# Moving the second layer's keys from the opening of a two-layer attention and mixture-of-experts kernel into its router and expert stages

## The reference, cut to what matters

```python
# x: [2, 512, 256]   ctx: [2, 1024, 256]   16 heads of 16
x = x + attention0(layernorm(x), ctx, mask)          # Wq0, Wk0, Wv0, Wo0 and biases
x = x + moe_capacity(layernorm(x))                   # router, top 2 of 8 experts, capacity 32 a group
x = x + attention1(layernorm(x), ctx, pad, attn_mask) # Wq1, Wk1, Wv1, Wo1 and biases
x = x + moe_top2(layernorm(x))                       # 8 experts, top 2
# in both attentions
q = y @ Wq.T + bq;  k = ctx @ Wk.T + bk;  v = ctx @ Wv.T + bv
out = softmax(mask(q k^T / 4)) v @ Wo.T + bo
```

## Time and profile before

| | |
|---|---|
| runs (3) | 1237.43, 1238.1 (median), 1240.68 us |
| the profiled execution | 1238.72 us, span 1237.0 us |
| busy | PE 1145.1, PEld 732.2, DVE 544.9, ACT 450.2, POOL 244.2 us |
| opening | 0 to 87 us |
| attention 0 with its projection | 88 to 340 us |
| router stage, expert stage | 341 to 380 us, 380 to 627 us |
| attention 1 with its projection, top-2 mixture | 628 to 941 us, 942 to 1237 us |

### The profile page before, as it was taken

One profiled execution on the slowest core, in us unless ns is written; L12 is line 12 of the kernel. 1 busy time (PEld: TensorE's weight loads), 2 busy tenths in 40 slices (PEclk: granted clock), 3 DMA queues, 4 the chain that ended last, 5 costly groups with the idle time before them and its releaser, 6 DMA issues. The chain is left out here.

```text
span 1237.0 us, 19157 instructions
## 1 busy us (share of the span) xinstructions
PE 1145.1 (93%) x7215; PEld 732.2 (59%) x7239; DVE 544.9 (44%) x1553; ACT 450.2 (36%) x591; POOL 244.2 (20%) x366
## 2 busy tenths in 40 slices
PE   6989999999859999999779999999987699999996
PEld 4443333333447888888656333333326699999995
DVE  4657777773362111121157776666406322212111
ACT  4556666666422111111143455555652101110110
POOL 4652222225000000000004000000200233333331
PEclk9999999999959999999989999999998799999998
DMA  8646222001172333345349221120004599999971
GB/s 224 166 150 159 42 40 43 3 1 50 53 273 51 136 136 136 136 147 195 65 180 210 38 39 39 40 40 1 1 1 160 202 372 377 314 321 310 318 231 47
DMA packets 87926, 168.53 MB, mean 136 GB/s; under 512 B 9474, under 2 KB 61396, under 8 KB 85252
## 3 DMA queue, kind: packets, MB, share of 16 engines
q1 hardware_dynamic: 80132, 157.99, 40.5%
q0 software_dynamic: 5152, 6.05, 2.5%
q10 hardware_dynamic: 2560, 3.41, 1.0%
HBM read 147.30 MB, written 20.98 MB: 136 GB/s over the span
## 5 line engine op out<-in xcount | busy, mean ns | idle before, releaser
L1213 ACT ACTIVATE prob<-st_ps 128x1024 f32<-128x1024 f32 x256 | 253.8, 1022 | 186.9 <-PE st_ps L1095 105.0
L219 DVE CUSTOM_DVE_ANT_0 junk<-s_ps,bias_rows,mx 128x512 f32<-128x512 f32 x236 | 167.8, 748 | 64.0 <-PE s_ps L204 63.3
L1087 PE MATMUL st_ps<-q_stack,k_stack 100*128 100x512 bf16 x512 | 183.7, 382 | 7.6 <-ACTq L1188 3.5
L219 DVE CUSTOM_DVE_ANT_0 junk<-s_ps,bias_rows 128x512 f32<-128x512 f32 x232 | 153.3, 689 | 66.0 <-PE s_ps L204 65.5
L204 PE MATMUL s_ps<-k_stack,q_stack 97*128 97x512 bf16 x468 | 174.9, 383 | 7.3 <-ACT q_stack L248 5.4
L1600 PE MATMUL h_ps<-expert_in,w 128*128 (+1 forms) x704 | 155.0, 382 | 2.2 <-PEq L66 2.2
L1600 PEld LDWEIGHTS h_ps<-expert_in,w 128*128 128x128 f32 (+1 forms) x704 | 132.7, 189 | 23.0 <-issue 2.4
L1107 PE MATMUL o_ps<-prob,v_unit 128*32 128x512 f32 x1024 | 139.7, 599 | 1.0 <-ACT prob L1213 1.0
L204 PEld LDWEIGHTS s_ps<-k_stack,q_stack 97*128 97x128 bf16 x468 | 44.8, 98 | 140.2 <-DVE mx L219 83.8
L1946 ACT ACTIVATE silu<-gu_ps 128x512 f32<-128x512 f32 x46 | 27.5, 597 | 227.1 <-PE gu_ps L1887 227.1
L1630 ACT ACTIVATE gelu_out<-h_ps 128x256 f32<-128x256 f32 (+1 forms) x88 | 33.7, 383 | 182.2 <-PE h_ps L1600 182.2
(11 more groups left out here) (283 smaller groups left out, 1185.3 us busy)
## 6 DMA issues: line engine op xcount, KB each, us to landing
wg<-in_gateT SPq DMA_DIRECT2D x23, 1024.0 KB
wu<-in_upT SPq DMA_DIRECT2D x23, 1024.0 KB
wd<-in_downT SPq DMA_DIRECT2D x23, 1024.0 KB
w<-in_w SPq DMA_DIRECT2D x16, 1368.0 KB
w<-in_w SPq DMA_DIRECT2D x8, 1280.0 KB
k_scr<-k_parts SPq DMA_DIRECT2D x48, 128.0 KB, 2.3
k_stack<-k_scr SPq DMA_DIRECT2D x16, 384.0 KB, 4.9
k_stack<-k_scr SPq DMA_DIRECT2D x16, 256.0 KB, 5.6
```

The costliest lines, as they stand in the source:

```text
L219: self.pr.nc.vector.tensor_tensor_reduce(out=self.junk[:, self.bank("job", u, j)], in0=self.ps[:, self.bank("job", u, j)], in1=self.m.bias ...
L1087: pe.matmul(st_ps[:, h], stack(K[b], ROWS, i % 2, h, slice(kt * P, (kt + 1) * P)), stack(Q[b], ROWS, i % 2, h, slice(0, SQ)), start=True, ...
L1213: nc.scalar.activation(prob[:, kt % 2, 2 * hp:2 * hp + 2], st_ps[:, 2 * hp:2 * hp + 2], ACT.Exp).then_inc(exp_done, 1)
```

## The change

The opening has 12 cells, with the second half of the queries as cells 6 and 7 and `NA = 8`; the first layer's last four key cells come in four rounds of five row jobs, one cell and one value tile, and four rounds of three jobs and two value tiles follow. Only 4 value tiles stand ahead of the loop (`OWN`), 12 are copied by ACT without bias, and POOL adds it later. Four row jobs of unit 1 (`EARLY`) are done ahead instead of 12. The second layer's key weights and `ctxT` are loaded in the last unit of attention 0 into buffers that are free by then (`K[0]`, `V[0]`), its 8 key cells are multiplied in the router stage between PE's other work, and POOL splits them in the expert stage, where SP sends them out and reads two stacks back before it loads the third expert's weights.

```diff
@@ opening, order of the cells
-        cells = [("k", 0, 0, 0), ("k", 0, 0, 1), ("q", 0, 0, 0), ("k", 0, 0, 2), ("k", 0, 0, 3), ("q", 0, 0, 1)]
-        cells += [("k", 0, 1, ch) for ch in range(4)] + [("q", 0, 1, 0), ("q", 0, 1, 1)]
-        cells += [("k", 1, dt, ch) for dt in range(DT) for ch in range(4)]
+        cells = [("k", 0, 0), ("k", 0, 1), ("q", 0, 0), ("k", 0, 2), ("k", 0, 3), ("q", 0, 1)]
+        cells += [("q", 1, 0), ("q", 1, 1)] + [("k", 1, ch) for ch in range(4)]
-        NA = 6
+        NA = 8
+        OWN = 4
-            return JOBS[PER * r:PER * (r + 1)] if r < NC - NA - 1 else JOBS[PER * r:]
+            return JOBS[5 * r:5 * r + 5] if r < 4 else JOBS[20 + 3 * (r - 4):23 + 3 * (r - 4)]
@@ opening, SP
-                sp.dma_start(wk_raw[1], t["wkT1"].rearrange("(t p) n -> p t n", p=P)).then_inc(wk_in[1], 16)
-                bias_in(sp, bk[:, 1], t["bk1"], wk_in[1])
...
-                for dt in range(DT):
-                    for b in range(B):
-                        for i in (2 * dt, 2 * dt + 1):
-                            k_out_of(1, i, b, 12 + 4 * dt + 2 * b + 1)
@@ opening, POOL, behind the last split
+                pool.wait_ge(v_kept, NV // 2 - OWN)
+                g.tensor_tensor(m.vals[:, OWN:NV // 2], m.vals[:, OWN:NV // 2],
+                                m.bv[:].unsqueeze(1).broadcast_to([P, NV // 2 - OWN, D]), ALU.add).then_inc(v_sum, 1)
+                top.cut(pool, row, 1)
@@ opening, PE
                 cell(5)
+                cell(6)
+                cell(7)
                 pe.wait_ge(wv_in, 32)
-                for n in range(NV // 2):
+                for n in range(OWN):
                     value(n)
...
-                    row.scores(pe, jobs[:1])
-                    cell(NA + r, (1,))
-                    row.scores(pe, jobs[1:])
+                    row.scores(pe, jobs[:2])
+                    cell(NA + r, (0,))
+                    row.scores(pe, jobs[2:4])
+                    cell(NA + r, (1,))
+                    row.scores(pe, jobs[4:])
+                    value(OWN + r)
+                for r in range(4):
+                    jobs = jobs_of(4 + r)
+                    row.scores(pe, jobs[:1])
+                    value(2 * OWN + 2 * r)
+                    row.scores(pe, jobs[1:])
+                    value(2 * OWN + 2 * r + 1)
+                    if r == 1:
+                        top.turn(pe, 0)
+                pe.wait_ge(pr.load[0][1], 16 * N_DMA)
+                row.scores(pe, NEXT[:3])
+                top.turn(pe, 1)
+                row.scores(pe, NEXT[3:])
+                pe.wait_ge(hi_done, NA + 2)
+                pe.wait_ge(full_done, 2)
+                for n in range(4):
+                    pe.matmul(kq_ps[:, 0, 0:D], pr.ident[:], ctxT[:, 0, 0:D], start=True, stop=True)
@@ attend, layer 0
-        plan = row_plan(AHEAD if l == 0 else 0)
+        plan = row_plan(EARLY if l == 0 else 0)
@@ attend, SP, layer 0
+                    sp.wait_ge(st_ready, (NU - 1) * 16)
+                    sp.dma_start(pr.late_ctx(), t["ctxT"].rearrange("(t p) n -> p t n", p=P)).then_inc(pr.late_in, 16)
+                    sp.wait_ge(pv_done, 2 + (NU - 1) * KT)
+                    sp.dma_start(pr.late_wk()[0], t["wkT1"].rearrange("(t p) n -> p t n", p=P)).then_inc(pr.late_in, 16)
+                    bias_in(sp, pr.late_bk, t["bk1"], pr.late_in)
                     sp.wait_ge(cut_done, KT)
@@ moe_capacity, router stage, PE
+                    key_cell(0)
+                    key_cell(1)
                     norm.tensor(pe, tps, logits)
+                    key_cell(2)
+                    key_cell(3)
                     pe.wait_ge(m1_done, 1)
@@ moe_capacity, router stage, ACT
+                    def key_out(n):
+                        act.wait_ge(k_ready, n + 1)
+                        bias = pr.late_bk[:, n // 4:n // 4 + 1]
+                        nc.scalar.activation(pr.late_part(n, 0), kps[:, n % 3], ACT.Identity, bias=bias)
+                        nc.scalar.activation(pr.late_full(n), kps[:, n % 3], ACT.Identity, bias=bias).then_inc(full_done, 1)
-                    norm.scalar(act, tps)
+                    norm.scalar(act, tps, first_keys)
                     act.wait_ge(x_sub, 1)
                     nc.scalar.activation(raw[:], raw[:], ACT.Exp).then_inc(x_exp, 1)
+                    for n in range(2, NK):
+                        key_out(n)
@@ moe_capacity, expert stage, SP
+                for dt in range(DT):
+                    for b in range(B):
+                        sp.wait_ge(late_low, 4 * dt + 2 * b + 2)
+                        for i in (2 * dt, 2 * dt + 1):
+                            keys_out(pr, sp, 1, pr.late_parts(), pr.late_out, i, b)
+                sp.wait_ge(pr.late_out, 16 * 3 * NG * B)
                 for b in range(B):
                     k_stack(pr, sp, 1, 0, b)
@@ moe_capacity, expert stage, POOL (new)
+                def split(n):
+                    rest = pr.late_full(n)
+                    g.tensor_tensor(rest, rest, pr.late_part(n, 0), ALU.subtract).then_inc(late_step, 1)
+                    pool.wait_ge(late_step, 2 * n + 1)
+                    g.tensor_copy(pr.late_part(n, 1), rest).then_inc(late_step, 1)
+                    pool.wait_ge(late_step, 2 * n + 2)
+                    g.tensor_tensor(pr.late_part(n, 2), rest, pr.late_part(n, 1), ALU.subtract).then_inc(late_low, 1)
```

More of the change, by code:

```diff
@@ L399, in split_done, with k_out_of @@
                     sp.wait_ge(lo_done, n + 1)
-                def k_out_of(l, i, b, last):
+                def k_out_of(i, b, last):
                     split_done(last)
-                    keys_out(pr, sp, l, k_parts, k_out[l], i, b)
+                    keys_out(pr, sp, 0, [k_parts[:, p] for p in range(3)], k_out[i][b], i, b)
                 def q_out_of(i, b, last):
@@ L481, in cell @@
                 def cell(n, ks=range(DT)):
-                    kind, l, dt, ch = cells[n]
-                    w, src = (wk[:, l], ctxT) if kind == "k" else (wq, pr.yT)
+                    kind, dt, ch = cells[n]
+                    w, src = (wk, ctxT) if kind == "k" else (wq, pr.yT)
                     for k in ks:
@@ L626, in _ @@
                         middle(n - 1)
-                    if n - NA == 10:
+                    value_kept(OWN + n - NA)
+                middle(NC - 1)
+                for n in range(2 * OWN, NV):
+                    value_kept(n)
+                    if n == 2 * OWN + 4:
                         top.write(act, 0)
-                middle(NC - 1)
                 top.write(act, 1)
@@ L692, in _ @@
                 dve.wait_ge(wv_in, 32)
-                for n in range(NV // 2):
+                for n in range(OWN):
                     value_out(n)
-                for r in range(NC - NA):
+                for r in range(8):
                     row.maxima(dve, jobs_of(r))
-                for n in range(NV // 2, NV):
-                    value_out(n)
+                row.maxima(dve, NEXT)
 class NormSteps:
@@ L808, in q_stack, with keys_out @@
                      src[:, 0:n]).then_inc(pr.load[l][b], 16)
-def keys_out(pr, sp, l, parts, done, i, b):
+def keys_out(pr, eng, l, parts, done, i, b):
     dst = scratch(pr, "k_scr", l, i, b, SK)
@@ L815, in keys_out @@
     for p in range(3):
-        sp.dma_start(dst[:, p], parts[at:at + HG * DH, p, i // 2, b * SK:(b + 1) * SK]).then_inc(done[i][b], 16)
+        eng.dma_start(dst[:, p], parts[p][at:at + HG * DH, i // 2, b * SK:(b + 1) * SK]).then_inc(done, 16)
 def queries_out(pr, sp, l, m, i, b):
@@ L1431, in logits, with key_cell @@
                         mm.then_inc(l_ready, 1)
+                    def key_cell(n):
+                        dt, ch = divmod(n, 4)
+                        if n == 0:
+                            pe.wait_ge(pr.late_in, 64)
+                        if n >= 3:
+                            pe.wait_ge(full_done, n - 2)
+                        for k in range(DT):
+                            mm = pe.matmul(kps[:, n % 3], wk[:, k, dt * P:(dt + 1) * P],
+                                           ctx[:, k, ch * 512:(ch + 1) * 512], start=(k == 0), stop=(k == DT - 1))
+                        mm.then_inc(k_ready, 1)
+                    key_cell(0)
+                    key_cell(1)
                     norm.tensor(pe, tps, logits)
+                    key_cell(2)
+                    key_cell(3)
                     pe.wait_ge(m1_done, 1)
```

156 lines of the change are left out of this document (100 added, 56 removed).

## The result

The changed kernel took 1226.6 us (median of four runs, 1220.6 to 1228.1) against 1238.1 before: a ratio of 0.9883 with a 95% interval of 0.9862 to 0.9903. Two later series gave 0.9865 (0.9841 to 0.9890) and 0.9873 (0.9847 to 0.9898). Forecast were 1224 us, a range of 1217 to 1231, and a gain of over 0.3% with a chance of 93%. The profiled execution took 1228.0 us (span 1226.3, against 1237.0 of before).

The account below looks back on a forecast made before the run. PE, or chains through it, was taken to bound the opening and attention, while the router stage had room. Terms 0.7 - 15.4 + 1.75 - 0.9 + 0 - 0.5 + 0 = -14.3 us gave 1224 us, range 1217 to 1231.

Parts of the forecast that it names:

- Part 1: Opening ahead of the loop: two more query cells delay the third value tile; cost 0.7 us, between 0 and 2.
- Part 2: Opening's loop and tail: 33.3 us in place of 48.7, so -15.4 us, bounds -10 and -17.
- Part 3: Attention: eight more row jobs in unit 0 cost 1.75 us, less half clock at its start saves 0.9.
- Part 4: Attention's end: late loads on SP's queue, some 17 us, cost nothing; if late, up to 5 us.
- Part 5: Router stage: key cells between PE's other work, earlier logits, faster dispatch; sum -0.5 us.
- dispatch itself: Router stage: dispatch matmuls, 9.81 us before, are 6.9 at full clock, but DVE feeds them every 1.2 us: -1.9.
- The -4.6 of a full clock: Router stage: the gain in us if the clock stayed full throughout; as a rival, 17%, total 1220 us.
- rows 9: Profile rows of the second mixture's router stage: clock falls to 0.52 amid transposes and logits though PE counts as busy.
- Part 6: Expert stage: POOL's splits and SP's sends delay the third expert's weights, with 5 us of slack: cost nothing.
- The slower-side rival: Expert stage: POOL at half speed, splits take 51 us, third expert's weights late, PE waits 20 us: 1244 us; 4%.

Follow-up runs that it names:

- DVE's other order: Changed kernel with DVE's row bias behind the first two value outputs and ahead of the last two, not ahead of all four; 1225.1 us, ratio 0.9879.
- the thin cells: Kernel before the change, the second layer's eight key cells in the opening multiplying 8 columns instead of 512; 1240.0 us against 1242.4, ratio 0.9988.
- the 2, 2, 2, 2 order: The changed kernel's own placement of the router stage's eight key cells, two in each of four places, the first ahead of the transposes; 1226.6 us.
- the one profile with full clock throughout: Changed kernel with one key cell cut in halves inside the logits, then 1, 1, 2 cells and one inside dispatch; 1222.8 us.

## Why the prediction was right, point by point

The sum was -14.3 us, the profile has -10.7. The sign, the range and the mechanism of the large term held. The 3.6 us that are missing are 1.1 in part 1 (where the starts of the two profiles fell), 0.9 in part 2, 2.0 in part 5, and -0.1 and -0.2 in attention and behind the router stage.

- **Part 1, ahead of the loop (+0.7).** The third value tile waits for DVE by 3.60 us ("some 4"), and the two tiles behind it take 2.4 us and not 3.4. But the loop starts at 40.86, not 39.9, as the first value tile is at 32.95 and 30.7 was expected (27.25 of before and two cells). The mean of the first value tile's start is 31.6 us over the twelve profiles with the changed opening and 28.2 over the two of before's (27.25 and 29.19): 3.4 apart, which is what two cells at full clock take. So the 2.25 us are no cost of the change but where the two profiles fell in the spread of the start. One profile of each kernel can't carry a term of 1 us here. The wait was a real cost, and one that the term rightly named: DVE's other order took 1.4 to 1.7 us off at the same clock.
- **Part 2 (-15.4).** Loop to attention 34.26 us (33.9 and 34.0 in the later profiles), forecast 33.3. The chain was right: four rounds in 17.4 us (17.1), of which the first, at half clock, had 4.8 and the others 4.2 on average, then four rounds and the turn in 10.7 (10.7). The miss is in the tail, 4.4 + 1.1 forecast and 6.2 measured from the first of unit 1's jobs (68.91): the four filling matmuls end the stage, 1 us behind ACT, which the term took as parallel; without them attention starts 0.8 us earlier. That PE's work alone wouldn't give the gain was only implied by the chain; the thin cells point the same way.
- **Part 3 (+0.85).** +0.73. Without fillers +1.73: so the 1.75 us for eight jobs and the 0.9 of half clock are both right in size (5 times 0.2 is 1.0, which is what the fillers saved).
- **Part 4 (0).** Right: projection to router stage is 15.63 us in both.
- **Part 5 (-0.5), the term that was wrong.** +1.52, and of the other sign. Two of its steps failed. The first is the clock in the cells. The logits were 1.15 us earlier (forecast 1.3), but the step "two cells partly at half clock make the first small matmul 0.8 late" measured 2.8: the clock was at half for nearly all of both, and back to full from the fifth cell on, where the third or fourth had been assumed. The later waits took a part of that up again, and dispatch started 2.25 us later in its stage, where the steps of the forecast add up to 1.4. The second is dispatch itself, -1.9 forecast and -0.73 measured with the clock at full. The term had named what paces it, DVE every 1.2 us, but didn't use it: seven such steps and a last group of 0.9 are 9.3 us, 0.5 less than before's 9.81, and 9.05 were measured. The -4.6 of a full clock never showed with the 2, 2, 2, 2 order; the one profile with full clock throughout, with the cells in other places, had a stage 2.1 us shorter than before's. Besides, the first cells took 5.4 us in four of six profiles with that order and put the transposes 1.9 us late; 0.3 had been allowed. Two of the forecast's own signs failed with it: the clock at 1.0 from the third or fourth cell, and dispatch within 2 us of its place. By the Trainium skill, "TensorE: Matmul & The Clock Gate", Part 1, activity should have kept the clock; the row at 340 to 342 us has PE busy all the time at 0.51, so the measurement decides, as it did for rows 9.
- **Part 6 (0).** Right, with 6.6 to 7.7 us of slack where 5 were forecast. A split took 3.0 us, each of POOL's two subtractions in it 1.15 beside DVE's multiplications of the experts. The slower-side rival's condition is real, but it begins only when SP reaches the weights some 7 us later than it does, and its reading of POOL's 2.41 us as half speed is wrong. In the profile with DVE's other order the same operation beside the row bias took 3.07 us:

```profile
36.30 2.28 DVE L732 TENSOR_SCALAR bias_rows<-mask_rows 128x4096 bf16<-128x4096 uint8 x1
36.53 3.07 POOL L473 TENSOR_TENSOR q_parts<-kq_rest,q_parts 128x512 bf16<-128x512 f32 x1 [0.87 <-ACT q_parts L623]
```

It began earlier in DVE's 2.28 us and ended 1.0 us behind DVE's end, as it did before (32.75 against 31.74) and after (39.07 against 38.06). So the operation took what was left of DVE's and 1.0 us more, which half speed doesn't give (by it 1.9 and 2.2 us in place of 2.41 and 3.07). That agrees with the lock of the Trainium skill, "SBUF — State Buffer", SBUF: two separate sides.

The total alone tells little of the terms. Its median is 2.6 us above the forecast, one and the same kernel spreads over 8 us, and the range would have taken in a router stage 4 us worse still.

## What to carry to other kernels

Before work is taken from a busy engine in a loop, thin it (same rounds, same waits, 8 columns): where the other engines are at 90%, as DVE and POOL were here, little of it comes back, and the rounds themselves have to go. Before a matmul block is priced by the clock, look at what feeds it: dispatch, fed by DVE every 1.21 us, took 9.05 us at full clock and with a third of it at half. When a variant is compared by stage, compare profiles with the same clock at its start: of 2.9 us between two openings only 1.4 to 1.7 were the order's. Work moved into holes is sized at the slow clock, hole by hole: here one cell behind the logits in place of two, and three ahead of dispatch, turned a stage 1.5 us longer than before into one 0.7 to 3.5 us shorter. A load's slack is worth measuring by delaying it on purpose, since past its end PE pays for the wait and again for the clock.

## What the hardware showed that was not expected

- Two kernels with the same instructions up to that point, alike to 0.02 us from the first value tile on, got a full clock in one and half in the other 1.1 us after the same 1.94 us standstill had ended; of ten profiles with full-size cells and that standstill it fell in five, 0.2 to 1.1 us into the stage.
- In ten of the eleven profiles in which the clock was at full as the logits began, it fell to half for 3 to 10 us while PE worked without a pause on them, on the transposes among them (one) or on the first cell behind them (two, within 0.4 us). The exception had long matmuls among the short ones.
- POOL's operation beside DVE's row bias took 2.41 or 3.07 us by when it began in it, and ended 1.0 us behind DVE's end each time.
- The first microseconds differ by as much as any stage: the first value tile is at 29.3 to 33.6 us for the same code, where PE could begin on `ctxT`'s first columns at 8.9 to 10.8 us and half clock fell in other places. From the first expert to the end it was 853.3 to 858.3 us in the eleven profiles with the same work there. All 15 runs of the changed kernel lie between 1220.5 and 1229.0 us, and a median of five of them can't resolve 2 us.
